# A perceiver layer's attention: TensorE's matmuls split into two streams of 64 rows, and its program written out step by step

## The chip, the core and the metric

One core of a Trainium2 chip runs the whole kernel. The core has five engines that run their own programs and wait for one another through semaphores: TensorE (PE; its weight loads are shown apart, as PEld), VectorE (DVE), ScalarE (ACT), GpSimd (POOL) and SyncE (SP), which here issues all DMAs. The metric is the device time of one execution in microseconds (us); lower is better.

## The reference, cut to what matters

The layer is cross attention, then a recurrent token mixing, then a feed-forward block, each added to the residual. The change touches the attention alone: 32 batches, 64 queries and 1601 context rows of 192 channels each, 16 heads of 64.

```python
q = query @ w_q                      # 32 x 64 x 1024
k, v = split(context @ w_kv)         # 32 x 1601 x 1024 each
scores = einsum('bhqd,bhkd->bhqk', q, k) * 64 ** -0.5
attn = softmax(scores, axis=-1)
out = einsum('bhqk,bhkd->bhqd', attn, v) @ w_out + b_out
x = x + out
```

The kernel never forms k and v. It multiplies the queries by the key weights first (192 channels for each of 16 x 64 head-and-query rows), so the scores are a product of these rows with the raw context, and the attention's output is the probabilities times the raw context, 192 wide, with the value weights applied later. Every operand is held as a high and a low part, and a product is a sum of terms of high and low parts.

## The kernel before, in words

Four stages follow one another: `write_queries` (queries times key weights, to a DRAM scratch), `attend_batches` (the attention), `attention_output` and `mix_and_feed`. The change is in `attend_batches`, which is named p2 in the source.

`attend_batches` takes 256 steps, 8 for each batch; a step handles 128 of the batch's 1024 head-and-query rows. Every engine runs its own program: a first pass of 16 steps, a loop of 14 passes of 16 steps, and a last pass of 16 (`passes`). The order on each engine is fixed by its program.

- TensorE, step s: `step_scores` (L757 to L776), then `product` for step s-4 (L778 to L793). The scores of a step are 128 x 1602, in four banks of PSUM, held once. They are cut into four chunks of 288, 512, 512 and 290 columns, and each chunk is a sum of five matmuls over 128 rows: query parts high and low with channels 0 to 127 of the context's high part, query high with the context's low part, and query high and low with a tile whose rows 0 to 63 are channels 128 to 191 of the high part and whose rows 64 to 127 are the same channels of the low part (the query tile repeats its 64 channels in both halves). The first chunk waits until ScalarE has read the left half of the last scores (`exp_left`), the third until it has read the rest (`exp_done`). The product is 13 tiles of 128 context rows; for each tile the transposed probabilities' high part meets 384 columns (the context's high and low part side by side) and their low part meets 192. Its sums lie in `acc`, one bank for each of two steps in turn.
- VectorE, step s: the maximum of the left half (L714), of the right half (L716), both combined (L719); then for step s-5 the scaled sum of the two halves of `acc` (L695) and its transposition into `o_t` (L701); then, once ScalarE has written the exponentials, their transposition into `turned` (L725), and the reciprocal of the row sums (L726, L728).
- ScalarE, step s: the high part of the landed probabilities of step s-4 (L614, two calls; waits for the end of the product of step s-5, since `pt_hi` and `pt_lo` exist once); the scaled second half of `acc` of step s-5 into `part` (L605); one piece of preparing the next batch; then the two exponentials of step s (L646).
- GpSimd, step s: the low part of the probabilities of step s-4 (L550, two calls), and one piece of preparing the next batch (L558, L562, L569, L577).
- SyncE: for every two steps 16 DMAs that move `turned` into `landed` (L485, `move`), and each batch's loads and stores between them.

## Time and profile before

| | |
|---|---|
| median of 3 runs | 2573.53 us (2570.07 to 2574.76) |
| the profiled execution's own time | 2574.86 us |
| its span, first to last instruction | 2573.1 us |
| mean granted TensorE clock | 0.958 |
| busy: PE, PEld, DVE, ACT, POOL | 2355.1, 2145.3, 1710.9, 1516.0, 1700.7 us |
| 256 steps of the attention, first to last maximum | 170.7 to 2059.3 us of the span |

The page's section 2 shows 40 slices of the span with the busy share of each engine; from the fifth to the thirty-second slice TensorE's digit is 9 throughout at full granted clock. Matmuls are pipelined, so the durations of single matmuls overlap: their rate is read from start to start. The waits and the idle times name the instruction that ended them. A line such as L773 is a line of the kernel before.

### The profile page before, as it was taken

To read this page: it belongs to the slowest core of one execution; us is meant where nothing else is said; L and a number is where in the kernel's file an instruction comes from. 1 tells how busy PE (TensorE), PEld (TensorE's weight loads), DVE (VectorE), ACT (ScalarE), POOL (GpSimd) and SP (SyncE) were. 2 spreads that over 40 slices of the span, in tenths; PEclk is the share of its full clock that TensorE was granted. 3 is DMA by queue.
4 is the path that set the end of the run, shared out by engine and by line. 5 is a ranking of instruction groups with operands and counts; after the bars stand their busy time and mean duration, and the time that the engine had idled before them with its cause. 6 is when DMAs were issued, how large, how long until landed. Compare 5 with 4: busy or idle time off the path is not lost. (4 is left out here: it accounts for less than half of the span.)

```text
span 2573.1 us, 43052 instructions
## 1 busy us (share of the span) xinstructions
PE 2355.1 (92%) x13872; PEld 2145.3 (83%) x13872; DVE 1710.9 (66%) x2666; ACT 1516.0 (59%) x2459; POOL 1700.7 (66%) x873
## 2 busy tenths in 40 slices
PE   4969999999999999999999999999999947855777
PEld 3649999999999999999999999999999945744666
DVE  7766666666666666666666666666666626768762
ACT  4646666666666666666666666666666525543342
POOL 2007788888888888888888888888888632023452
PEclk9989999999999999999999999999999968986888
DMA  5957878888788888888777788878888549910000
GB/s 158 259 155 190 193 193 198 194 192 193 194 192 195 199 194 195 197 198 197 192 193 195 192 193 200 196 192 199 196 198 195 131 102 219 187 50 0 9 9 17
DMA packets 387378, 434.18 MB, mean 169 GB/s; under 512 B 45652, under 2 KB 362232, under 8 KB 387320
## 3 DMA queue, kind: packets, MB, share of 16 engines
q1 hardware_dynamic: 387320, 433.45, 69.2%
q8 instruction: 32, 0.52, 0.1%
q14 instruction: 26, 0.21, 0.0%
HBM read 162.73 MB, written 52.43 MB: 84 GB/s over the span
## 5 line engine op out<-in xcount | busy, mean ns | idle before, releaser
L550 POOL TENSOR_TENSOR p_pt_lo<-p_landed,p_pt_hi 128x768 fp32r<-128x768 f32 (+1 forms) x512 | 1005.1, 1985 | 359.9 <-ACT p_pt_hi L614 359.9
L789 PE MATMUL p_acc<-p_nat,p_pt_hi 128*128 128x384 f32 x3328 | 978.5, 362 | 14.1 <-POOL p_pt_lo L550 13.8
L791 PE MATMUL p_acc<-p_nat,p_pt_lo 128*128 128x192 f32 x3328 | 845.7, 254 | 0.0
L646 ACT ACTIVATE p_prob<-p_scores,p_negmax 128x800 f32<-128x800 f32 (+1 forms) x512 | 471.2, 926 | 515.7 <-DVE p_negmax L719 515.7
L773 PE MATMUL p_scores<-p_ct_hi,p_q_hi 128*128 128x512 f32 (+2 forms) x2048 | 710.2, 350 | 24.2 <-DVE p_ct_hi L746 13.8
L773 PE MATMUL p_scores<-p_ct_hi,p_q_lo 128*128 128x512 f32 (+2 forms) x2048 | 705.1, 348 | 0.0
L725 DVE STREAM_TRANSPOSE turned<-p_prob 128x1664 f32<-128x1664 f32 x256 | 489.5, 1912 | 317.0 <-ACT p_prob L646 317.0
L789 PEld LDWEIGHTS p_acc<-p_nat,p_pt_hi 128*128 128x128 f32 x3328 | 630.7, 190 | 16.5 <-issue 13.7
L791 PEld LDWEIGHTS p_acc<-p_nat,p_pt_lo 128*128 128x128 f32 x3328 | 640.8, 193 | 0.0
L614 ACT ACTIVATE p_pt_hi<-p_landed 128x768 fp32r<-128x768 f32 (+1 forms) x512 | 432.3, 892 | 159.2 <-PE p_acc L791 152.5
L773 PEld LDWEIGHTS p_scores<-p_ct_hi,p_q_hi 128*128 128x128 f32 x2048 | 388.8, 190 | 71.9 <-issue 14.3
L773 PEld LDWEIGHTS p_scores<-p_ct_hi,p_q_lo 128*128 128x128 f32 x2048 | 390.7, 191 | 44.7
L716 DVE TENSOR_REDUCE p_halfmax<-p_scores 128x1 f32<-128x801 f32 x256 | 254.1, 993 | 212.7 <-PE p_scores L773 212.7
L773 PE MATMUL p_scores<-p_ct_lo,p_q_hi 128*128 128x512 f32 (+2 forms) x1024 | 354.2, 346 | 0.0
L714 DVE TENSOR_REDUCE p_halfmax<-p_scores 128x1 f32<-128x800 f32 x256 | 253.7, 991 | 59.5 <-PE p_scores L773 52.3
L773 PEld LDWEIGHTS p_scores<-p_ct_lo,p_q_hi 128*128 128x128 f32 x1024 | 194.3, 190 | 22.3
L577 POOL TENSOR_TENSOR p_nat<-shared,p_nat 128x1152 fp32r<-128x1152 f32 (+1 forms) x62 | 178.5, 2879 | 0.0
L562 POOL TENSOR_TENSOR p_q_lo<-p_stage,p_q_hi 128x1024 fp32r<-128x1024 f32 x62 | 148.5, 2395 | 15.2 <-ACT p_q_hi L624 15.2
L695 DVE SCALAR_TENSOR_TENSOR p_o_q<-p_acc,p_rinv,p_part 128x192 f32<-128x192 f32 x256 | 107.0, 418 | 35.3 <-ACT p_part L605 34.4
L605 ACT ACTIVATE p_part<-p_acc,p_rinv 128x192 f32<-128x192 f32 x256 | 103.0, 402 | 31.4 <-PE p_acc L791 31.4
L558 POOL TENSOR_TENSOR p_ct_lo<-p_stage,p_ct_hi 128x802 fp32r<-128x802 f32 (+1 forms) x62 | 109.5, 1767 | 14.2 <-ACT p_ct_hi L621 14.2
L569 POOL TENSOR_TENSOR p_ct_hi<-p_stage,p_ct_hi 64x802 fp32r<-64x802 f32 (+1 forms) x62 | 109.0, 1757 | 5.6 <-POOL p_pt_lo L550 0.5
(190 smaller groups left out, 2652.9 us busy)
## 6 DMA issues: line engine op xcount, KB each, us to landing
p_landed<-turned SPq DMA_DIRECT2D x2048, 104.0 KB, 2.2
shared<-in_ctx SPq DMA_DIRECT2D x96, 312.0 KB
o_scratch<-shared SPq DMA_DIRECT2D x256, 96.0 KB, 2.6
qk_scratch<-p_out_a SPq DMA_DIRECT2D x16, 1024.0 KB, 4.6
p_oa<-o_scratch SPq DMA_DIRECT2D x32, 512.0 KB, 6.0
p_stage<-qk_scratch SPq DMA_DIRECT2D x31, 512.0 KB, 3.9
p_stage<-qk_scratch SPq DMA_DIRECT2D x62, 256.0 KB, 4.2
p_stage<-in_ctxT SPq DMA_DIRECT2D x31, 401.0 KB, 3.2
```

What stands on the lines that cost most here:

```text
L550: nc.gpsimd.tensor_tensor(pt_lo[:, t0:t1, :, :], by_tile(slot, t0, t1), bits(pt_hi[:, t0:t1, :, :]), ALU.subtract).then_inc(pt_lo_done, 1)
L558: nc.gpsimd.tensor_tensor(ct_lo[1 - par][:, lo:hi], stage[:, u, 0:hi - lo], bits(ct_hi[1 - par][:, 0, lo:hi]), ALU.subtract).then_inc(ct_a ...
L562: nc.gpsimd.tensor_tensor(stepped(q_lo[1 - par][:, u - 3, :]), by_step(stage[:, u - 3, :]), bits(stepped(q_hi[1 - par][:, u - 3, :])), ALU ...
L577: nc.gpsimd.tensor_tensor(x[:, t0:t1, DC:2 * DC], raw[:, t0:t1, :], bits(x[:, t0:t1, 0:DC]), ALU.subtract).then_inc(nat_done, 1)
L614: nc.scalar.activation(pt_hi[:, t0:t1, :, :], by_tile(slot, t0, t1), ACT.Copy).then_inc(pt_hi_done, 1)
L646: nc.scalar.activation(prob[:, lo:hi], scores[:, S0 + lo:S0 + hi], ACT.Exp, bias=negmax[:, par:par + 1], accum_out=rowsum[:, par, h:h + 1] ...
L714: nc.vector.tensor_reduce(halfmax[:, par, 0:1], scores[:, S0:S0 + MID], AX.X, ALU.max, negate=True).then_inc(halfmax_done, 1)
L716: nc.vector.tensor_reduce(halfmax[:, par, 1:2], scores[:, S0 + MID:S0 + NKV], AX.X, ALU.max, negate=True).then_inc(halfmax_done, 1)
L725: nc.vector.transpose(turned[:, j % 4, :], prob[:, :]).then_inc(turned_done, 1)
L773: last = nc.tensor.matmul(scores[:, S0 + lo:S0 + hi], w, x, start=m == 0, stop=m == len(terms) - 1)
L789: nc.tensor.matmul(acc[k % 2][:, 0:2 * DC], pt_hi[:, t, :, :].rearrange("p i x -> p (i x)"), x[:, t, :], start=t == 0, stop=False, skip_gr ...
L791: last = nc.tensor.matmul(acc[k % 2][:, 0:DC], pt_lo[:, t, :, :].rearrange("p i x -> p (i x)"), x[:, t, 0:DC], start=False, stop=t == KT - ...
```

## The change

It touches TensorE's program in `attend_batches`, and what feeds and drains it.

- Scores: the chunks are now 400, 400, 400 and 402 columns, a bank each, and the halves are 800 and 802 columns. A matmul covers 64 rows only: one on rows 0 to 63 (UPPER) into one chunk, and beside it one on rows 64 to 127 (LOWER) into the other chunk of the pair. `passes_of` writes such pairs out: for each pair of chunks five on "their own" halves, then, after a wait for these (`own_done`), four on the crossed halves. The fifth term of the crossed pass (query low with the context's low part of channels 128 to 191) is left out. The order is: own of the left pair, own of the right pair, crossed left (then `left_ready`), crossed right (then `scores_ready`). That makes 36 matmuls for a step in place of 20.
- For this, the tile of channels 128 to 191 holds high and low parts in rows that alternate from chunk to chunk (`ROWS_B`): GpSimd writes the low part in two pieces of 400 columns for each half, and the counts of `ct_b_done` double.
- Product: each of the 26 matmuls becomes two, on rows 0 to 63 and on rows 64 to 127, into two banks: `acc` is now `[P, 2, 512]`, twice. 52 matmuls for a step in place of 26.
- Draining `acc`: VectorE sums its four parts (2 banks x 2 halves of 192) in one `tensor_reduce` of 768 elements, as the first instruction of its step (`sum_out`); ScalarE scales the sum (`scale_out`, now waiting for VectorE and reading SBUF), and VectorE transposes it where it did before (`turn_out`). The old scaled sum (L695) goes.
- TensorE's program is written out for all 256 steps; the other engines keep their loops.

```diff
-HALVES = [(0, 802), (802, NKV + NKV % 2)]
+HALVES = [(0, 800), (800, NKV + NKV % 2)]
...
+    C = HALVES[1][0] // 2
+    CHUNKS = [(0, C), (C, 2 * C), (2 * C, 3 * C), (3 * C, CW)]
+    CHALF, MID = HALVES, HALVES[1][0]
+    PLACE = [512 - C, 512, 3 * 512 - C, 3 * 512]
+    UPPER, LOWER = slice(0, DCB), slice(DCB, P)
+
+    ROWS_B = [(UPPER, LOWER), (LOWER, UPPER)]
...
-        acc = [pb(f"acc{i}", [P, 512]) for i in range(2)]
+        acc = [pb(f"acc{i}", [P, 2, 512]) for i in range(2)]
...
-                    dst = ct_hi[1 - par][DCB:P, 1, lo:hi]
-                    nc.gpsimd.tensor_tensor(dst, stage[DCB:P, u - 6, 0:hi - lo], bits(dst), ALU.subtract).then_inc(ct_b_done, 1)
-                    pool.wait_ge(ct_b_done, n * 2 + (u - 3))
+                    for c in (2 * (u - 6), 2 * (u - 6) + 1):
+                        (c0, c1), rows = CHUNKS[c], ROWS_B[c % 2][1]
+                        dst = ct_hi[1 - par][rows, 1, c0:c1]
+                        nc.gpsimd.tensor_tensor(dst, stage[rows, u - 6, c0 - lo:c1 - lo], bits(dst), ALU.subtract).then_inc(ct_b_done, 1)
+                    pool.wait_ge(ct_b_done, n * 4 + (2 * u - 6))
...
-            def half_out(p, ring, par, fresh):
-
-                act.wait_ge(acc_ready, p + 1)
+            def scale_out(p, ring, fresh):
+
+                act.wait_ge(acc_read, p + 1)
                 act.wait_ge(rinv_done, p + 1)
                 if not fresh:
 
-                    act.wait_ge(acc_read, p)
-                nc.scalar.activation(part[:, :], acc[par][:, DC:2 * DC], ACT.Copy, scale=rinv[:, ring:ring + 1]).then_inc(part_done, 1)
+                    act.wait_ge(o_done, p)
+                nc.scalar.activation(o_q[:, :], o_sum[:, :], ACT.Copy, scale=rinv[:, ring:ring + 1]).then_inc(o_scaled, 1)
...
+            def sum_out(r, j, first):
...
+                dve.wait_ge(acc_ready, p + 1)
...
+                parts = acc[k % 2][:, :, 0:2 * DC].rearrange("p b (h c) -> p c b h", c=DC)
+                nc.vector.tensor_reduce(o_sum[:, :], parts, AX.XY, ALU.add).then_inc(acc_read, 1)
...
             def step(r, j, first):
                 s, par = r * SPP + j, j % 2
+                sum_out(r, j, first)
                 dve.wait_ge(left_ready, s + 1)
...
-                drain(r, j, first)
+                turn_out(r, j, first)
                 dve.wait_ge(exp_done, s + 1)
...
+                def passes_of(chunk_pair, count, own):
+
+                    for m in range(count):
+                        w, x = terms[m]
+                        for rows, c in zip((UPPER, LOWER), chunk_pair):
+                            lo, hi = CHUNKS[c]
+                            last = nc.tensor.matmul(scores[:, PLACE[c]:PLACE[c] + hi - lo], w[rows], x[rows, lo:hi], start=own and m == 0,
+                                                    stop=not own and m == count - 1, skip_group_check=True)
+                    return last
+
+
+                for h in range(2):
+                    if not (first and j == 0):
+
+                        pe.wait_ge(exp_done if h else exp_left, s)
...
+                    passes_of((2 * h, 2 * h + 1), len(terms), True).then_inc(own_done, 1)
+                for h in range(2):
+                    pe.wait_ge(own_done, s * 2 + (h + 1))
+                    passes_of((2 * h + 1, 2 * h), len(terms) - 1, False).then_inc(scores_ready if h else left_ready, 1)
...
+                        for w, width in ((pt_hi, 2 * DC), (pt_lo, DC)):
+                            for i, rows in enumerate((UPPER, LOWER)):
+                                last = nc.tensor.matmul(acc[k % 2][:, i, 0:width], w[rows, t, :, :].rearrange("p i x -> p (i x)"),
+                                                        x[rows, t, 0:width], start=t == 0 and w is pt_hi, stop=t == KT - 1 and w is pt_lo,
+                                                        skip_group_check=True)
...
-            passes(pe, body)
+            for r in range(NB // SPB):
+                body(r, r == 0, r == NB // SPB - 1)
```

## Rows read from the trace of the kernel before

**Rows 1.** Windows, 705 to 1185 us: us, busy by engine (instructions), clock, DMA

```profile
705.00:1185.00 480.00, 480.00 (x2991) 451.60 (x2991) 324.18 (x521) 313.44 (x521) 395.61 (x195) 1.00 0.80 195
```

**Rows 2.** Waits, 400 to 2100 us: engine, line, releaser, us in total, times, longest

```profile
POOL p_pt_lo L550 <- ACT p_pt_hi L614: 320.4, 229, 6.2
DVE p_halfmax L716 <- PE p_scores L773: 187.2, 225, 0.9
```

**Rows 3.** Timeline of PE around one step: start us, duration, line, operation, tiles

```profile
1000.08 0.40 PE L773 MATMUL p_scores<-p_ct_hi,p_q_lo 128*128 128x512 f32 x1
...
1002.18 0.30 PE L773 MATMUL p_scores<-p_ct_hi,p_q_hi 128*128 128x290 f32 x1
...
1002.86 0.34 PE L789 MATMUL p_acc<-p_nat,p_pt_hi 128*128 128x384 f32 x1
...
1006.57 0.32 PE L773 MATMUL p_scores<-p_ct_hi,p_q_hi 128*128 128x288 f32 x1
...
1007.25 0.39 PE L773 MATMUL p_scores<-p_ct_hi,p_q_hi 128*128 128x512 f32 x1
```

**Rows 4.** Timeline of DVE, one step in the steady stretch

```profile
1003.06 0.99 DVE L716 TENSOR_REDUCE p_halfmax<-p_scores 128x1 f32<-128x801 f32 x1 [0.74 <-PE p_scores L773]
...
1006.33 1.92 DVE L725 STREAM_TRANSPOSE turned<-p_prob 128x1664 f32<-128x1664 f32 x1 [1.23 <-ACT p_prob L646]
...
1008.31 0.16 DVE L728 RECIPROCAL p_rinv<-p_rowtot 128x1 f32<-128x1 f32 x1
...
1010.44 0.99 DVE L716 TENSOR_REDUCE p_halfmax<-p_scores 128x1 f32<-128x801 f32 x1 [0.84 <-PE p_scores L773]
```

**Rows 5.** The maxima of the scores, all steps: duration min/median/max, first and last start

```profile
L716 DVE TENSOR_REDUCE p_halfmax<-p_scores x256: 974/992/995, 171.6 to 2059.3; 128x1 f32<-128x801 f32 x128
```

**Rows 6.** Timeline of PEld (weight loads) in the product of the same step

```profile
1003.04 0.19 PEld L789 LDWEIGHTS p_acc<-p_nat,p_pt_hi 128*128 128x128 f32 x1
1003.15 0.19 PEld L791 LDWEIGHTS p_acc<-p_nat,p_pt_lo 128*128 128x128 f32 x1
```

**Rows 7.** Timeline of PE in the first stage: four short matmuls in a row

```profile
40.69 0.60 PE L300 MATMUL p_tp<-p_ident,shared 128*128 128x128 f32 x4
```

**Rows 8.** DMA queues, the program's own instructions among them, 0 to 400 us

```profile
q8 instruction: 14, 0.23, 0.3%
```

**Rows 9.** Timeline of ACT after that product: start, duration, [idle before]

```profile
1006.77 1.69 ACT L614 ACTIVATE p_pt_hi<-p_landed 128x768 fp32r<-128x768 f32 x2 [0.57 <-PE p_acc L791]
```

**Rows 10.** Timeline of POOL, the same time

```profile
1007.69 3.92 POOL L550 TENSOR_TENSOR p_pt_lo<-p_landed,p_pt_hi 128x768 fp32r<-128x768 f32 x2 [1.62 <-ACT p_pt_hi L614]
1011.57 1.61 POOL L558 TENSOR_TENSOR p_ct_lo<-p_stage,p_ct_hi 128x800 fp32r<-128x800 f32 x1
```

**Rows 11.** Timeline of DVE, first steps, where the scores were already there

```profile
170.70 0.98 DVE L714 TENSOR_REDUCE p_halfmax<-p_scores 128x1 f32<-128x800 f32 x1
171.60 0.97 DVE L716 TENSOR_REDUCE p_halfmax<-p_scores 128x1 f32<-128x801 f32 x1
...
193.36 0.16 DVE L728 RECIPROCAL p_rinv<-p_rowtot 128x1 f32<-128x1 f32 x1
193.44 0.97 DVE L714 TENSOR_REDUCE p_halfmax<-p_scores 128x1 f32<-128x800 f32 x1
```

**Rows 12.** Groups by line, whole span: instructions, busy us, mean ns, idle before

```profile
L695 DVE SCALAR_TENSOR_TENSOR p_o_q<-p_acc,p_rinv,p_part 128x192 f32<-128x192 f32 x256 | 107.0, 418 | 35.3 <-ACT p_part L605 34.4
L605 ACT ACTIVATE p_part<-p_acc,p_rinv 128x192 f32<-128x192 f32 x256 | 103.0, 402 | 31.4 <-PE p_acc L791 31.4
...
L637 ACT ACTIVATE p_nat<-shared 128x1152 fp32r<-128x1152 f32 (+1 forms) x62 | 76.7, 1237 | 0.0
```

**Rows 13.** Timeline of SP (DMA issues), one move of two steps

```profile
1030.40 10.41 SPq L485 DMA_DIRECT2D p_landed<-turned  x16
```

**Rows 14.** Waits of SP's DMA queue, 400 to 2000 us

```profile
SPq L480 <- DVE turned L725: 46.2, 53, 1.2
SPq L458 <- POOL p_ct_hi L569: 39.1, 26, 1.7
```

More of the change, by code:

```diff
@@ L650, in drain @@
                 if not (first and j < LAG + 1):
-                    half_out(r * SPP + (j - LAG - 1), (j - LAG - 1) % SB, (j - LAG - 1) % 2, first and j == LAG + 1)
+                    scale_out(r * SPP + (j - LAG - 1), (j - LAG - 1) % SB, first and j == LAG + 1)
             def raise_high(r, j, first):
@@ L688, in _, with turn_out @@
         def _(dve):
-            def out(p, ring, par, fresh_half, first):
-                dve.wait_ge(part_done, p + 1)
-                if not first:
-                    dve.wait_ge(o_done, p)
-                nc.vector.scalar_tensor_tensor(o_q[:, :], acc[par][:, 0:DC], rinv[:, ring:ring + 1], part[:, :], ALU.mult,
-                                               ALU.add).then_inc(acc_read, 1)
-                dve.wait_ge(acc_read, p + 1)
-                if fresh_half is not None:
-                    dve.wait_ge(stored[ring // (SB // 2)], fresh_half)
-                nc.vector.transpose(o_t[:, :, ring, :], o_q[:, :].rearrange("p (k x) -> p k x", x=R)).then_inc(o_done, 1)
-            def drain(r, j, first):
+            def sum_out(r, j, first):
+                if first and j < LAG + 1:
+                    return
+                k = j - LAG - 1
+                p = r * SPP + k
+                dve.wait_ge(acc_ready, p + 1)
+                if not (first and k == 0):
+                    dve.wait_ge(o_scaled, p)
+                parts = acc[k % 2][:, :, 0:2 * DC].rearrange("p b (h c) -> p c b h", c=DC)
+                nc.vector.tensor_reduce(o_sum[:, :], parts, AX.XY, ALU.add).then_inc(acc_read, 1)
+            def turn_out(r, j, first):
                 if first and j < LAG + 1:
@@ L707, in drain @@
                 ring, batch = k % SB, k // SB
-                fresh = ring % (SB // 2) != 0 or (first and batch == 0)
-                out(r * SPP + k, ring, k % 2, None if fresh else (r * SPB + batch) * (16 * G), first and k == 0)
+                dve.wait_ge(o_scaled, r * SPP + (k + 1))
+                if ring % (SB // 2) == 0 and not (first and batch == 0):
+                    dve.wait_ge(stored[ring // (SB // 2)], (r * SPB + batch) * (16 * G))
+                nc.vector.transpose(o_t[:, :, ring, :], o_q[:, :].rearrange("p (k x) -> p k x", x=R)).then_inc(o_done, 1)
             def step(r, j, first):
                 s, par = r * SPP + j, j % 2
+                sum_out(r, j, first)
                 dve.wait_ge(left_ready, s + 1)
-                nc.vector.tensor_reduce(halfmax[:, par, 0:1], scores[:, S0:S0 + MID], AX.X, ALU.max, negate=True).then_inc(halfmax_done, 1)
+                nc.vector.tensor_reduce(halfmax[:, par, 0:1], scores[:, PLACE[0]:PLACE[0] + MID], AX.X, ALU.max, negate=True).then_inc(halfmax_done, 1)
                 dve.wait_ge(scores_ready, s + 1)
-                nc.vector.tensor_reduce(halfmax[:, par, 1:2], scores[:, S0 + MID:S0 + NKV], AX.X, ALU.max,
+                nc.vector.tensor_reduce(halfmax[:, par, 1:2], scores[:, PLACE[2]:PLACE[2] + NKV - MID], AX.X, ALU.max,
                                         negate=True).then_inc(halfmax_done, 1)
@@ L752, in _ @@
             for j in range(LAG + 1):
-                drain(NB // SPB, j, False)
+                sum_out(NB // SPB, j, False)
+                turn_out(NB // SPB, j, False)
         @block.tensor
@@ L760, in step_scores @@
                     pe.wait_ge(q_done, b * 2 + 2)
-                q = lambda t, k: t[par][:, k, (j % SB) * P:(j % SB + 1) * P]
-                for c, (lo, hi) in enumerate(CHUNKS):
-                    if c % 2 == 0 and j % SB == 0:
-                        pe.wait_ge(ct_a_done, b * 2 + (c // 2 + 1))
-                        pe.wait_ge(ct_b_done, b * 2 + (c // 2 + 1))
-                    if c % 2 == 0 and not (first and j == 0):
-                        pe.wait_ge(exp_left if c == 0 else exp_done, s)
-                    ct_a, ct_b, ct_al = (t[:, lo:hi] for t in (ct_hi[par][:, 0, :], ct_hi[par][:, 1, :], ct_lo[par]))
-                    terms = ((q(q_hi, 0), ct_a), (q(q_lo, 0), ct_a), (q(q_hi, 0), ct_al), (q(q_hi, 1), ct_b), (q(q_lo, 1), ct_b))
-                    for m, (w, x) in enumerate(terms):
-                        last = nc.tensor.matmul(scores[:, S0 + lo:S0 + hi], w, x, start=m == 0, stop=m == len(terms) - 1)
-                    if c == 1:
-                        last.then_inc(left_ready, 1)
@@ L788, in product @@
                     for t in range(t0, t1):
-                        nc.tensor.matmul(acc[k % 2][:, 0:2 * DC], pt_hi[:, t, :, :].rearrange("p i x -> p (i x)"), x[:, t, :], start=t == 0, stop=False,
-                                         skip_group_check=True)
-                        last = nc.tensor.matmul(acc[k % 2][:, 0:DC], pt_lo[:, t, :, :].rearrange("p i x -> p (i x)"), x[:, t, 0:DC], start=False,
-                                                stop=t == KT - 1, skip_group_check=True)
+                        for w, width in ((pt_hi, 2 * DC), (pt_lo, DC)):
[3 more added lines that the diff above has]
+                                                        skip_group_check=True)
                 last.then_inc(acc_ready, 1)
```

34 lines of the change are left out of this document (18 added, 16 removed).

## The prediction

> **What bounds the kernel now.** I read the windows first. From 705 to 1185 us TensorE is busy for all 480 us at full granted clock, while VectorE has 324 us, ScalarE 313 us and GpSimd 396 us of work [rows 1]. The waits agree: GpSimd waits for ScalarE's high part and VectorE for the scores, while TensorE has no wait of weight in that stretch [rows 2]. So TensorE's pace is the pace of a step. The timeline shows what it is made of. From start to start, five matmuls of 288 columns take 1007.25 - 1006.57 = 0.68 us, that is 0.136 us each; nine of 512 take 1002.18 - 1000.08 = 2.10, that is 0.2333 each; the five of 290 take 0.68; the product's 13 tiles take 1006.57 - 1002.86 = 3.71, that is 0.2854 for a pair of 384 and 192 columns [rows 3]. The sum is 0.68 + 2.33 + 0.68 + 3.71 = 7.40 us; from one right-half maximum to the next it is 1010.44 - 1003.06 = 7.38 [rows 4]. All 256 steps run from 171.6 to 2059.3 us, 7.40 for one on average [rows 5], so this stage is 1888 us of the 2573.1.
>
> Two things in these rows matter for a cut into halves. A weight load costs 0.107 to 0.11 us from start to start (1003.04 to 1003.15) [rows 6], and four loads with matmuls of 128 columns come at the same pace: (0.60 - 0.27) / 3 = 0.11, taking 0.27 for the last one's own length [rows 7]. Under a matmul of 290 columns or more it hides; under one of 192 it does not quite. The excess over pure streaming is small everywhere.
>
> **TensorE after the change.** Scores: 18 pairs of 64-row matmuls of 400 columns. Between 0.136 at 288 and 0.2333 at 512 the slope is 0.000434 us for a column, so a full-height matmul of 400 columns would take 0.185 [rows 3]. If the two of a pair run side by side, a step's scores cost 18 x 0.185 = 3.33 us against 3.69 now: one tenth of the columns goes with the term that is left out, and two starts in twenty. The product keeps its columns: 26 pairs in place of 26 matmuls, 3.71 us. Sum 7.04. If the two run one after the other, it is twice that, 14.1. No row of before shows a matmul on half the rows, so these are the bounds. I take 7.04: the two use different rows of the array, different partitions of the operands and different banks, and no row shows something that they share except the order of issue and the port for weights.
>
> That port is the doubtful place. There are 88 loads in a step where there were 46. If the loads of both halves stand in one line at 0.107, a pair of the scores takes 0.214 (over 0.185) and a tile of the product 4 x 0.107 = 0.428 (over 0.285): 18 x 0.214 + 13 x 0.428 = 9.42 us. The same price comes out if the queue can't issue a load and a matmul faster than the 0.11 us of [rows 7]; that row can't say whether it shows a limit of the load or of the issue.
>
> The Trainium skill, TensorEngine Tiling (Array Packing), Key Properties, says that different tiles "can execute LdWeights and Matmul in parallel"; no run here shows it yet. By that rule the loads of the halves don't line up, and 7.04 stands. The skill's page TensorE: Matmul & The Clock Gate (Part 3, The mechanism) says that a load overlaps matmuls in flight only where the row groups differ. By that rule a full-height load could not hide now, and the split would gain all of it; the rows disagree, since loads of all 128 rows start 0.11 us apart under running matmuls [rows 6], so nothing is to be gained there.
>
> **TensorE's program, written out.** The loop's back edge costs nothing visible now, since TensorE is busy throughout [rows 1]. Written out, the program has to be fetched while it runs: in the first 400 us, 14 blocks of 16 KB came in [rows 8] for the written-out parts, and the mean step shows no room for a stall with each. A step has 88 matmuls and 88 loads in place of 46 and 46, so a block (256 instructions of 64 bytes) would last some 10 us in place of 20. I cost it at nothing, and at up to 1 us for a block (every 1.4 steps) if each one stalls: 0.7 us a step.
>
> **Who is next at 7.04.** Four loops of dependences close once in a step.
>
> GpSimd and ScalarE around the product. `pt_hi` and `pt_lo` exist once. The product ends at 1006.57, ScalarE starts at 1006.77 [rows 9], GpSimd at 1007.69, and the second low half is ready at 1011.61 [rows 10]: 5.04 us after the product's end. Then 7 of 13 tiles are left, 7 x 0.2854 = 2.00. The loop needs 7.04, and up to 0.1 more for the wake-ups.
>
> VectorE. Its chain goes from the right-half maximum over the maximum of both, ScalarE's exponentials and the transposition to the reciprocal: 1008.31 - 1003.06 = 5.25 us [rows 4]. The reciprocal to the next instruction, unwaited, is 0.08, and left-half to right-half maximum is 0.90 when the scores are there [rows 11]. Without any wait for TensorE that is 6.23, and this is why VectorE could wait 0.83 us in each step [rows 2, 4]. The change adds `sum_out` to that chain, in front. The scaled sum (0.42 us [rows 12]) that it replaces ran while VectorE waited 1.23 us for the exponentials anyway [rows 4], so its going gives nothing back. `sum_out` reads 768 elements of PSUM in one reduction; the nearest row is a reduction of 800, which occupies 0.90, so 0.87. Bounds: 0.42 below (no cheaper than the sum it replaces) and 4 x 0.42 = 1.67 above (each of four parts at the old price). The chain needs 6.23 + 0.87 = 7.10, with bounds 6.65 and 7.90. The skill's tiling page (PSUM Bottleneck) warns that a faster TensorE moves the limit to the draining of PSUM; that agrees with this sum, which alone gives the number.
>
> SyncE. A move of two steps takes 10.4 us of issue [rows 13] of 14.8. Over 1600 us its queue waited 46.2 + 39.1 us [rows 14], that is 0.39 for each of 217 steps: it can't go below 7.38 - 0.39 = 6.99.
>
> ScalarE has one new wait, `scale_out` on `sum_out`; queued behind it are a piece of preparation (up to 1.24 us [rows 12]) and the exponentials. `sum_out` ends 5.25 + 0.08 + 0.87 = 6.20 us after a right-half maximum, the scaling (0.40 [rows 12]) and the preparation end by 7.84, and the next exponentials are due at 7.10 + 1.2 = 8.3 (1.2 is 1006.33 - 1003.06 less the wait of 1.23 and twice 0.42 for L695 and the transposition behind it [rows 4, 12]). It has cover of about 0.4 us; if that were gone, the excess would go on VectorE's chain one for one. The split of GpSimd's low part for channels 128 to 191 adds two starts in a batch, hidden beside its idle time [rows 2].
>
> **The sum.** The loops need 7.04, 7.04 to 7.14, 7.10 and 6.99 us. The largest likely one is 7.10 to 7.14, and loops this close will jostle: I take 7.15. Against 7.38 that is 0.23 us for each of 255 steps, 59 us. The last step's drain gets 0.5 longer. Span 2573.1 - 58 = 2515; its own time lies 1.8 above the span, and the median of the runs 1.3 below that: 2515 for the median.
>
> **Rivals.**
> 1. *The other loops take the gain.* If the wake-ups, the fetches or a late DMA cost 0.1 to 0.25 us more, a step takes 7.25 to 7.4: 2545 to 2578 us. For it: four loops within 0.15 us. Against it: the mean of all steps now lies only 0.02 above a steady one [rows 4, 5], so stalls are rare.
> 2. *VectorE's new reduction is slow (the other side).* Place: `sum_out`, at the head of VectorE's step. It decides from 7.38 - 6.23 = 1.15 us upward. At its upper bound, 1.67, a step takes 7.90: 2573.5 + 255 x 0.52 = 2706 us. A partial overlap of the halves would look alike in time and reach 2700 to 2750.
> 3. *Loads or issue in one line (slower).* 9.42 us: 2573.5 + 255 x 2.04 = 3094 us.
> 4. *The change doesn't do what it says:* the halves exclude each other, 14.1 us, 2573.5 + 255 x 6.7 = 4280 us.
>
> **How the numbers follow.** My forecast (7.05 to 7.25 us a step, 2490 to 2545) has 0.67; rival 1 has 0.10, of which 0.03 lies within 0.2% of before; rival 2 with partial overlap 0.07, with 0.01 of it within 0.2%; rival 3 has 0.12 and rival 4 0.04. Bound 0.2% is about what a measurement of this kernel can tell from no change. Faster 0.67 + 0.07 = 0.74, same 0.04, slower 0.22. The range runs from 2480 (7.02 a step, TensorE alone) to 2690, past rival 1 and through most of rival 2: it leaves out rivals 3 and 4 and a rest, just under 2 in 10. Its own range is 2490 to 2545.
>
> **What would show it.** Right: the two matmuls of a pair start within a few hundredths of a us and pairs of 400 columns come every 0.18 to 0.19 us, tiles every 0.285; `sum_out` near 0.96 us by its row; VectorE's wait in front of L716's successor shrinks from 0.83 to under 0.1, and TensorE for the first time waits in each step, for GpSimd's low part or the exponentials, by about 0.1 us. Rival 1 shows as larger waits of TensorE, or gaps that the profile puts down to issue at even distances of one block. Rival 2 shows as a row of `sum_out` over 1.2 us with VectorE never waiting. Rival 3 shows as loads 0.107 apart without a gap, whichever half they are for, and pairs at 0.21; rival 4 as the second of each pair starting when the first is through. The prediction is wrong at its root if pairs don't overlap, and wrong in size if the loops' slack, which I read from single steps, isn't there.

## The result and the profile after

| | before | after |
|---|---|---|
| median of the runs | 2573.5 us | 2641.3 us (2639.0 to 2646.0, 4 runs) |
| profiled execution: time, span | 2574.9, 2573.1 us | 2639.0, 2637.2 us |
| ratio after : before | | 1.027, interval 1.0255 to 1.0285 |
| mean step, first to last right-half maximum | 7.40 us | (2116.5 - 170.4) / 255 = 7.63 us |
| TensorE busy, 705 to 1185 us | 480.0 us | 464.4 us |

The change is 68 us slower, where 58 us less was forecast. Of the 64 us by which the span grew, 58 lie between the first and the last of the 256 maxima.

TensorE does what was hoped. The timeline of TensorE in the scores of a step (start, duration, "x2" is one pair) shows the halves side by side:

```profile
1004.62 0.37 PE L782 MATMUL p_scores<-p_ct_hi,p_q_hi 64*128 64x400 f32 x2
1004.82 0.34 PE L782 MATMUL p_scores<-p_ct_hi,p_q_lo 64*128 64x400 f32 x2
1005.01 0.34 PE L782 MATMUL p_scores<-p_ct_lo,p_q_hi 64*128 64x400 f32 x2
...
1007.75 0.35 PE L782 MATMUL p_scores<-p_ct_hi,p_q_hi 64*128 64x400 f32 x2
```

From the start of the first pair to that of the last are 17 pairs in 3.13 us: 0.184 us for a pair (0.185 was taken from [rows 3]). But the engine is no longer busy throughout. The windows view of 705 to 1185 us (columns as in [rows 1]) has 15.6 us without a matmul, and GpSimd and ScalarE do less work in the same time, so fewer steps:

```profile
705.00:1185.00 480.00, 464.38 (x5562) 443.68 (x5564) 337.35 (x505) 311.08 (x505) 387.71 (x207) 1.00 0.78 191
```

The waits of 400 to 2100 us (as [rows 2]: us in total, times, longest) have one kind that was next to nothing before, ScalarE's high part waiting for the landing of a move; TensorE's new waits come behind it. Before, then after:

```profile
ACT p_pt_hi L614 <- DMA p_landed<-turned: 1.7, 2, 1.0
```

```profile
ACT p_pt_hi L619 <- PE p_acc L813: 173.6, 144, 3.9
ACT p_pt_hi L619 <- DMA p_landed<-turned: 130.7, 79, 3.3
DVE p_halfmax L722 <- PE p_scores L782: 89.6, 163, 1.6
...
PEld p_acc L813 <- issue: 78.7, 88, 2.6
PE p_acc L813 <- POOL p_pt_lo L553: 54.0, 60, 2.3
```

SyncE's own queue, 400 to 2000 us, had 46.2 and 39.1 us of waiting before [rows 14] and has half of that now, although it has no issue more to make:

```profile
SPq L483 <- DVE turned L733: 20.0, 24, 1.1
SPq L488 <- POOL p_pt_lo L553: 16.7, 36, 0.7
SPq L461 <- POOL p_ct_hi L574: 4.3, 7, 2.8
```

One stall in full, around 410 us, on SyncE, ScalarE, GpSimd and TensorE ([idle before <- what ended it]):

```profile
395.55 1.98 SPq L497 DMA_DIRECT2D o_scratch<-shared  x4
397.76 11.53 SPq L488 DMA_DIRECT2D p_landed<-turned  x16
...
412.20 1.69 ACT L619 ACTIVATE p_pt_hi<-p_landed 128x768 fp32r<-128x768 f32 x2 [2.46 <-DMA p_landed<-turned]
413.12 3.89 POOL L553 TENSOR_TENSOR p_pt_lo<-p_landed,p_pt_hi 128x768 fp32r<-128x768 f32 x2 [3.15 <-ACT p_pt_hi L619]
415.06 0.21 PEld L813 LDWEIGHTS p_acc<-p_nat,p_pt_hi 64*128 64x128 f32 x2 [1.74 <-issue]
415.09 0.44 PE L813 MATMUL p_acc<-p_nat,p_pt_hi 64*128 64x384 f32 x2 [1.44 <-POOL p_pt_lo L553]
```

The move's sixteen issues take 11.53 us where one took 10.41 before [rows 13]. It lands late, ScalarE has idled 2.46 us, GpSimd 3.15, and TensorE stands for 1.44 us. What the profile puts down to "issue" for TensorE is mostly this: the weight load beside that matmul has the same gap under that name, and of the 76 us that such loads waited from 400 to 2000 us, 66 stand beside a matmul's wait for GpSimd's low part.

A long stand has a second price. Five times between 400 and 2000 us the granted clock falls to half (1.2 in place of 2.4 GHz) for 3.4 us, each time within 1.5 us behind a stand of TensorE of 1.7 to 2.3 us (four other stands of 1.8 to 2.1 us brought none). That is 17 us at half clock, where the kernel before has none in this stretch, and so at most some 9 us of the loss.

What lengthens the issues is in the page's third section, the queue by which the program's own instructions come in blocks of 16 KB. Before, then after:

```profile
q8 instruction: 32, 0.52, 0.1%
```

```profile
q8 instruction: 192, 3.15, 0.6%
```

Between 400 and 2000 us it is 3 blocks before (all behind 1950 us, near the last pass) and 145 after, one in 11 us. In the same stretch 143 of SyncE's DMA issues took over 0.7 us (4 before), in total 110 us over the usual 0.602 (2 before), and they begin 0.16 us (median) behind the start of a block: nearly every block lengthens one issue, by 0.8 us on average. The distribution of the move's issues (ns, minimum/median/maximum) shows it as a maximum only, since nine of ten are untouched:

```profile
L488 SPq DMA_DIRECT2D p_landed<-turned x1677: 585/602/1903, 399.8 to 1999.3; - x187
```

### The profile page after: what moved, and what is told of

It reads as the page before. It is cut to its first block and busy times, and to the rows that moved or that the text cites. A ratio compares the mean times of both kernels' runs of the same rounds, so it can differ in the third digit from the quotient of the medians.

```text
span 2637.2 us, 64213 instructions
## 1 busy us (share of the span) xinstructions
PE 2345.9 (89%) x24624; PEld 2169.6 (82%) x24624; DVE 1800.6 (68%) x2668; ACT 1542.9 (59%) x2459; POOL 1712.8 (65%) x935
## 3 DMA queue, kind: packets, MB, share of 16 engines
q8 instruction: 192, 3.15, 0.6%
## 5 line engine op out<-in xcount | busy, mean ns | idle before, releaser
L813 PE MATMUL p_acc<-p_nat,p_pt_hi 64*128 64x384 f32 x6656 | 1038.6, 370 | 84.7 <-POOL p_pt_lo L553 80.3
L813 PE MATMUL p_acc<-p_nat,p_pt_lo 64*128 64x192 f32 x6656 | 883.7, 252 | 0.0
L813 PEld LDWEIGHTS p_acc<-p_nat,p_pt_hi 64*128 64x128 f32 x6656 | 671.7, 188 | 165.4 <-issue 108.6
L782 PE MATMUL p_scores<-p_ct_hi,p_q_hi 64*128 64x400 f32 (+1 forms) x4096 | 689.5, 346 | 24.3 <-DVE p_ct_hi L755 14.1
L813 PEld LDWEIGHTS p_acc<-p_nat,p_pt_lo 64*128 64x128 f32 x6656 | 680.8, 191 | 0.0
L782 PE MATMUL p_scores<-p_ct_hi,p_q_lo 64*128 64x400 f32 (+1 forms) x3072 | 547.2, 343 | 0.0
L782 PEld LDWEIGHTS p_scores<-p_ct_hi,p_q_hi 64*128 64x128 f32 x4096 | 402.0, 185 | 26.7 <-issue 15.1
L782 PE MATMUL p_scores<-p_ct_lo,p_q_hi 64*128 64x400 f32 (+1 forms) x2048 | 363.6, 342 | 0.0
L782 PEld LDWEIGHTS p_scores<-p_ct_hi,p_q_lo 64*128 64x128 f32 x3072 | 307.4, 187 | 0.0
L705 DVE TENSOR_REDUCE p_o_sum<-p_acc 128x192 f32<-128x768 f32 x256 | 244.8, 956 | 52.8 <-PE p_acc L813 46.3
```

Source lines behind the costliest of these rows:

```text
L705: nc.vector.tensor_reduce(o_sum[:, :], parts, AX.XY, ALU.add).then_inc(acc_read, 1)
L782: last = nc.tensor.matmul(scores[:, PLACE[c]:PLACE[c] + hi - lo], w[rows], x[rows, lo:hi], start=own and m == 0, stop=not own and m == cou ...
L813: last = nc.tensor.matmul(acc[k % 2][:, i, 0:width], w[rows, t, :, :].rearrange("p i x -> p (i x)"), x[rows, t, 0:width], start=t == 0 and ...
```

## The experiments

Theory A: the blocks by which the written-out program is fetched lengthen SyncE's DMA issues, and through late landings the steps. Its rivals, by the letters that the expectations use: B (each block stalls TensorE itself; from e6 on the same is called D, which also takes in any other harm of a block), and C (the halves or the new draining are at fault, for instance because closely matched loops jostle, and writing out costs nothing). Ratios are to the kernel before on the same chip.

### Writing out, alone and taken back

e1: the changed kernel, TensorE in a loop of 16 steps again.

```diff
-            for r in range(NB // SPB):
-                body(r, r == 0, r == NB // SPB - 1)
+            passes(pe, body)
```

> The changed kernel with TensorE's loop put back (14 passes of 16 steps), all else kept. Theory A: the blocks of TensorE's written-out program that are fetched while it runs hold up SyncE's DMA issue (146 blocks between 400 and 2000 us, 143 issues of over 0.7 us there, 118 us more than 0.602 us each), and SyncE's line of issues is what a step waits for. If the loop's body of some 2900 instructions stays in place, the blocks and the long issues go, a step takes the 7.2 to 7.3 us of the undisturbed steps, and the kernel 2530 to 2550 us. If the body is fetched anew in each pass, the blocks stay at 0.69 a step and the time at 2640, which says nothing against A. Theory B, that each block stalls TensorE itself and SyncE's delay only follows from the longer step: the same time as A, but with the long issues still there. Theory C, the halves or the new reduction cost the time, not the fetches: 2640 with the blocks gone.

Measured: 2711.7 us, 1.055 (1.053 to 1.057), slower still. The loop doesn't take the blocks away: there are 230. Its body of 16 steps has 16 x 176 = 2816 matmuls and loads where that of before has 16 x 92 = 1472, and the 176 blocks that come between 400 and 2000 us say that it is fetched anew in each pass. New is a wait of TensorE at the back edge, about twice in a pass (waits, 400 to 2100 us):

```profile
PEld p_scores L782 <- issue: 79.6, 26, 4.2
PE p_scores L782 <- issue: 71.0, 26, 3.8
```

The stands at the back edge also bring stretches at half the granted clock, 99 us in the 1600 from 400 to 2000 us. So writing out was better than the loop for this body, by 70 us, and the experiment says nothing against A.

e2: the kernel before with TensorE's program written out, and nothing else (the same edit the other way round).

> The kernel before, with TensorE's program written out for all steps and nothing else changed. 93 instructions a step make 0.36 blocks a step. Theory A: each block makes one DMA issue some 0.8 us longer, 0.29 us a step, which fits into the 0.39 us a step that SyncE's queue waited before: the step stays at 7.38 to 7.42 us, the kernel at 2573 to 2590 us, and SyncE's waits shrink to about 0.1 us a step. Theory B, a block stalls TensorE by 0.5 to 1 us: TensorE is the bound here, so 93 blocks cost 45 to 90 us, 2620 to 2665 us. Theory C: no change, 2573.

Measured: 2591.1 us, 1.0069 (1.0052 to 1.0086): 18 us for the writing out alone. 108 blocks in all, 77 of them between 400 and 2000 us, 72 issues of SyncE over 0.7 us, and ScalarE waits for landings (waits, 400 to 2100 us):

```profile
ACT p_pt_hi L614 <- DMA p_landed<-turned: 46.9, 37, 3.0
```

C, by which writing out is free (2573), and B (2620 to 2665) are both out. A's size fits, 1 us above its range.

### The stores off SyncE's queue

e3 (changed kernel), e6 (e2), e7 (before) and e8 (e5, below): the eight stores of a batch are issued by ScalarE, one behind the exponentials of each step.

```diff
-                    if not begins:
-                        store(n - 1, 0)
...
                     step(r, j, first)
+                    store_after(n, u, begins, first and j == SB)
```

> The changed kernel, written out as it is, but the 8 stores of each batch to the scratch are issued by ScalarE, one behind the exponentials of each step, in place of SyncE. Theory A: SyncE's line gets 8 issues of 0.48 us shorter for a batch, 0.49 us a step, so it needs 7.46 - 0.49 = 6.97 to 7.1 and the other loops decide: 7.25 to 7.35 us a step, 2540 to 2570 us, although as many blocks are fetched as before. Theory B: 2640, since TensorE's own stalls stay. Theory C: 2640.

> The kernel before (full-height matmuls), TensorE's program written out as in e2_before_written_out, and the eight stores of each batch issued by ScalarE in place of SyncE. Theory A: the blocks come as in e2, but SyncE's queue has lost 8 issues of some 0.6 us in a batch of 59 us, so its spare grows from 61 to some 180 us in 1600 and the stalls shrink: 2573 to 2583 us, against 2591 with the stores on SyncE. Theory D (a block holds TensorE itself, whatever SyncE does): as e2, 2588 to 2594 us.

> Control: the kernel before with its loop and with the eight stores of each batch issued by ScalarE. SyncE had spare and TensorE was busy throughout in the kernel before, so theories A and D both expect no change: 2570 to 2577 us. Were it faster by more than 5 us, the stores on SyncE would cost something of their own, and e3 and e6 would not speak on the fetches alone.

Measured: e3 2595.7 us, 1.0083 (1.0063 to 1.0102), 46 us less than the changed kernel with the same 192 blocks, where B and C expected no gain; e6 2583.9 us, 1.0036 (1.0023 to 1.0049), 7 us less than e2; e7 2570.0 us, 0.9987 (0.9977 to 0.9998), so the place of the stores as such is worth 3 us at most. SyncE now waits 135 us of 1600 in e3, thus has spare, and landings are still late (78.5 us). e6 came 1 us above A's range and e3 26 above it: spare in the queue isn't enough. That led to the slack of the single move, below.

### The scores alone in halves

e4: the product with 128 rows and the old draining; scores in halves; written out.

```diff
-                        for w, width in ((pt_hi, 2 * DC), (pt_lo, DC)):
-                            for i, rows in enumerate((UPPER, LOWER)):
...
...
+                        nc.tensor.matmul(acc[k % 2][:, 0:2 * DC], pt_hi[:, t, :, :].rearrange("p i x -> p (i x)"), x[:, t, :], start=t == 0, stop=False,
```

> The changed kernel with the scores in halves, but the product with matmuls over all 128 rows into one bank, and its two halves scaled and added by ScalarE and VectorE as before the change (no reduction of 768). Written out. 62 matmuls a step, 0.49 blocks. Theory A: SyncE needs 6.99 + 0.49 x 0.83 = 7.40 us a step, so 2575 to 2590 us. Theory B (TensorE 7.04 plus 0.49 blocks at 0.5 to 1 us): 7.3 to 7.5, 2550 to 2605, with the waits on TensorE's side. Theory C, the reduction on VectorE is what costs: VectorE's chain is back at 6.23, TensorE at 7.04 to 7.1, 2500 us. If going from 64-row to 128-row matmuls and back twice a step costs TensorE anything, its gaps show at the two borders of a product.

Measured: 2601.4 us, 1.0107 (1.009 to 1.0124). That is 11 us above A's range, and far above the 2500 that stood for a reduction at fault. With 140 blocks it lies between e2 and the changed kernel, but its undisturbed step is 7.39 us, not the 7.04 that the streams add up to. The weight loads show where it goes, at the first load of each kind:

```profile
1001.65 0.19 PEld L778 LDWEIGHTS p_scores<-p_ct_hi,p_q_hi 64*128 64x128 f32 x2 [0.16 <-issue]
1005.13 0.19 PEld L807 LDWEIGHTS p_acc<-p_nat,p_pt_hi 128*128 128x128 f32 x1 [0.27 <-issue]
```

Those two gaps a step are not in the changed kernel, where everything has 64 rows. From start to start each of the two borders costs the matmuls about 0.18 us, together the 0.35 us that were missing. The Trainium skill, TensorEngine Tiling (Array Packing), Key Properties, says "Mode switching requires drain"; the trace agrees, at about 0.16 and 0.27 us.

### The same work without the blocks

e5: the changed kernel with TensorE in a loop of 8 steps (1408 matmuls and loads), which needs fixed buffers. It leaves out the turning of the buffers: TensorE computes every batch from the first batch's context and queries, so its output is not the layer's. Number and shape of instructions, waits and transfers are kept. The same holds for its descendants e8, e12, e14 and e18.

```diff
...
-                          (q_hi[par][:, 0, at], ct_lo[par]), (q_hi[par][:, 1, at], ct_hi[par][:, 1, :]),
...
+                          (q_hi[0][:, 0, at], ct_lo[0]), (q_hi[0][:, 1, at], ct_hi[0][:, 1, :]),
...
-            for r in range(NB // SPB):
-                body(r, r == 0, r == NB // SPB - 1)
+            batch(0)
+            with pe.Fori(1, NB) as b:
+                batch(b)
```

> The changed kernel with its halves, but TensorE's program is a loop over batches again, with a body of one batch (8 steps, some 1500 instructions, as long as the body that stayed resident in the kernel before). To make this possible TensorE reads the context and the queries always from the first of their two buffers while all writers write the second, so every batch is computed from the first batch's context and queries; the number and shape of all instructions, waits and transfers is that of the changed kernel. Theory A (the 16 KB blocks by which TensorE's written-out program is fetched lengthen SyncE's DMA issues, and SyncE's queue is then too slow for the moves): no blocks between 400 and 2000 us, no DMA issue over 0.7 us, moves of 10.3 us, steps of 7.1 to 7.3 us with few stalls, 2525 to 2555 us. Theory C (the stalls belong to the halves: closely matched loops jostle once a step takes 7.1 us, whatever is fetched): blocks gone, stalls as in the changed kernel, 2620 to 2650 us.

> e5_short_loop with the eight stores of each batch issued by ScalarE (again every batch uses the first batch's context and queries). Theory A in its plain form: without fetches SyncE needs 7.0 us a step and VectorE 7.1 to 7.2, so the relief moves little: within 15 us of e5, at 2520 to 2550 us. If SyncE were the bound at 7.1 us even without fetches (theory A2), it would be faster than e5 by over 15 us.

Measured: e5 2547.1 us, 0.9903 (0.9886 to 0.9919); e8 2549.6 us. Same halves, same draining, same transfers, 94 us less than the changed kernel and 26 less than before. From 400 to 2000 us there is no block of TensorE's queue, no stretch at half clock, no issue of a move over 0.672 us, and in the waits of 400 to 2000 us those for landings are gone:

```profile
ACT p_pt_hi L619 <- DMA p_landed<-turned: 2.4, 3, 0.9
```

This settles C against A: all 94 us hang on how TensorE's program is fetched. It also gives the price of a step without it, 7.27 us on the mean of 255, and e8 shows that SyncE's load isn't what sets these 7.27 (A2 is out).

How little a block must cost to matter is read from SyncE's and ScalarE's timelines of e5:

```profile
1186.95 0.54 SPq L468 DMA_DIRECT2D p_stage<-in_ctxT  x1
1187.72 10.35 SPq L488 DMA_DIRECT2D p_landed<-turned  x16
...
1200.45 1.69 ACT L619 ACTIVATE p_pt_hi<-p_landed 128x768 fp32r<-128x768 f32 x2 [0.68 <-PE p_acc L813]
```

The last of the sixteen is issued from 1197.46 to 1198.07. The trace has its landing at 1200.1, and ScalarE starts at 1200.45, so this move behind loads has 0.3 us of slack, and a block in it adds 0.8. Over all moves from 400 to 2000 us the time from the last landing to ScalarE's start is 0.9 us at the median in e5, and under 0.35 in one of ten; in the kernel before it is 1.3 and 0.9. That goes with what a block costs in the two: 18 us for e2's 108 blocks, 0.17 each, and 94 for the changed kernel's 192, 0.49 each.

### A shorter move, all blocks kept

e9, e11 and e12: the changed kernel, the kernel before and e5, with 4 of a move's 16 DMAs issued by ScalarE behind the exponentials of the next step (e10: and the stores too).

```diff
-                for i in range(G):
+                for i in range(G if whole else G - 1):
...
                     step(r, j, first)
+                    move_rest(r, j, first)
```

> The changed kernel (halves, TensorE's program written out, its 192 blocks as before), with 4 of the 16 DMAs of every move issued by ScalarE behind the exponentials of the step that follows, and 12 by SyncE. Theory A, made more precise: a block costs time only because it lengthens a DMA issue of a move, and the move of two steps (11 to 11.7 us of issue and 2.5 us to land, of 14.5 us) then lands after ScalarE wants it; TensorE itself is never short of instructions. Then a move that is issued in some 8 to 9 us absorbs its blocks: ScalarE's wait for the landing falls from 131 us to under 25 in 1600, the steps are 7.1 to 7.3 us, and the time is 2545 to 2560 us, all blocks still there. Theory D (a block also starves TensorE or slows something else): 2590 to 2620 us, with TensorE's waits put down to issue as large as in the changed kernel (74 us).

> Control: the kernel before (loop, full-height matmuls) with 4 of the 16 DMAs of every move issued by ScalarE. TensorE is busy throughout there, so both theories expect no change: 2569 to 2577 us.

> e5_short_loop (halves, TensorE's loop of 8 steps, so no blocks; every batch computed from the first batch's context and queries) with 4 of the 16 DMAs of every move issued by ScalarE. If GpSimd's and ScalarE's loop around the product is what sets 7.26 us without fetches, and not the moves: within 5 us of e5, 2542 to 2552 us. If the moves' latency set it, 2515 to 2535 us.

> As e9_move_quarter_on_act, and the eight stores of each batch on ScalarE's queue as well. Theory A: SyncE's queue has then 62 issues in a batch where it had 86, nothing is late, and the time is within 10 us of e9: 2543 to 2556 us. If the order of the stores among the moves still made landings late in e9, this one is faster than e9 by over 10 us. Theory D: 2585 to 2615 us.

Measured: e9 2603.3 us (1.0118), e11 2598.8 (1.0109), e12 2577.1 (1.0013); e10 2728.2 (1.062). In e9 the waits for landings are gone from the list, but the controls e11 and e12, which were expected to stay as they were, are 27 and 30 us slower than without the edit. ScalarE's queue and its work in e12:

```profile
1209.63 1.26 ACTq L646 DMA_DIRECT2D p_landed<-turned  x2
...
1211.57 0.63 ACTq L646 DMA_DIRECT2D p_landed<-turned  x1
1212.31 1.69 ACT L619 ACTIVATE p_pt_hi<-p_landed 128x768 fp32r<-128x768 f32 x2 [0.93 <-PE p_acc L827]
```

The issues run beside the exponentials, but the next instruction of ScalarE starts only behind the fourth, 0.10 us behind its end in each of the 108 moves from 400 to 2000 us, and four reach just past the point at which the high part is due: it starts 0.57 us behind the product's last matmul, 0.35 in e5. A block now lengthens these, and holds ScalarE (e9, waits of 400 to 2000 us, a kind that e12 does not have):

```profile
ACT p_pt_hi L619 <- issue: 28.7, 14, 2.5
```

So the comparison of e9 with e12 (26 us) could not tell A from D. e10 was expected within 10 us of e9 and came 125 above: with a store behind the four, ScalarE waited 190 us of 1600 for its own issues.

e13 to e15 had the same four as two in each of two steps:

> The changed kernel, written out, with 4 of the 16 DMAs of a move issued by ScalarE, but now two behind the exponentials of each of the two steps that follow, in place of four behind those of the first. In e12 the four took 2.5 us from the first exponential's start, 0.1 to 0.2 us past the point at which ScalarE wants to begin the next high part; two take 1.25 us (some 2.1 with a block), which the exponentials (1.95 us) and the wait behind them cover. Theory A (late landings are the only link between the blocks and the time): no landing is late, ScalarE is not held, 2547 to 2565 us with all 192 blocks, thus faster than the kernel before. Theory D (the blocks also hold TensorE, or another engine): 2585 to 2610 us.

> Control without blocks: e5_short_loop (TensorE's loop of 8 steps; every batch computed from the first batch's context and queries) with the same placement as e13. Covered as worked out there: 2543 to 2553 us, like e5 (2547). Were it like e12 (2577), ScalarE's issues cost time by their number, wherever they stand.

> Control: the kernel before with the same placement. If it is covered, 2570 to 2578 us; if ScalarE's issues cost time by their number, 2590 to 2600 us, as with four behind one step (2599).

Measured: e13 2784.9 us (1.083), e14 (as e5) 2714.4 (1.055), e15 (as before) 2732.5 (1.062). My placement was wrong: the second pair is issued a step later and lands late even without blocks (182 us of waits for landings in e14). They tell nothing on A and D, but show what late landings cost: e14 lies 167 us above e5, with 53 of 1600 us at half the granted clock.

e16: only 2 of the 16 on ScalarE, both in the first step. e17 and e18 (as e5) have the stores on ScalarE as well, two in each odd step.

```diff
-                    for g in range(G):
+                    for g in range(G if whole or i < G - 1 else 2):
...
+                for g in range(2, G):
...
+                    act.dma_start(dst, turned[i * R:(i + 1) * R, slots, g * GK:(g + 1) * GK]).then_inc(moved[par], 16)
```

> The changed kernel, written out, with 2 of the 16 DMAs of a move issued by ScalarE behind the exponentials of the first step that follows, 14 by SyncE. Without blocks (e5) a move that stands behind loads ends its issue at 1198.07 us, lands some 2.3 us later, and ScalarE's high part starts at 1200.45: a slack of about 0.1 us, and a block (+0.8 us) is late in full. With 14 issues the move ends 1.3 us earlier, and a block fits into the slack. ScalarE's two take 1.25 us (2.1 with a block) from the first exponential, 2.6 us ahead of the next high part. SyncE's queue: 78 issues of 0.65 and 5.5 blocks of 0.8 us are 55 of 58 us. Theory A: 2555 to 2580 us. Theory D (the blocks cost time in another way too): 2600 to 2625 us.

> As e16_move_eighth_on_act, and the eight stores of a batch too are issued by ScalarE, two in each odd step, so that ScalarE has two issues in every step and SyncE 70 in a batch, 46 us and 4.4 us of blocks of 58. Theory A: 2548 to 2565 us with all 192 blocks, faster than the kernel before (2573). Theory D: 2590 to 2620 us.

> Control of e17 without blocks: TensorE's loop of 8 steps (every batch computed from the first batch's context and queries), with e17's placement of the issues. ScalarE's two issues are covered in each step: 2542 to 2552 us, like e5 (2547). If it is above 2560, the placement has a price of its own, which is to be taken off e17.

Measured: e16 2553.8 us, 0.993 (0.9908 to 0.9951): 88 us less than the changed kernel, 21 less than before, and 7 above e5. It has all the blocks (first line, page), and the same lengthening of issues: from 400 to 2000 us 121 of SyncE's took over 1.0 us, 127 in the changed kernel. But SyncE is through with a move 1.3 us sooner, and hardly a landing is late (waits, 400 to 2000 us):

```profile
q8 instruction: 192, 3.15, 0.6%
```

```profile
1189.62 9.07 SPq L488 DMA_DIRECT2D p_landed<-turned  x14
```

```profile
ACT p_pt_hi L619 <- PE p_acc L827: 142.4, 204, 2.0
...
ACT p_pt_hi L619 <- DMA p_landed<-turned: 19.6, 15, 2.0
PEld p_acc L827 <- issue: 17.1, 41, 1.3
```

That decides A against D: 192 blocks cost 94 us where a move behind loads has 0.3 us of slack and 7 us where it has 1.3 more, and TensorE's "issue" waits and the stretches at half clock go with them. One control is missing: no run has e16's placement without the blocks. The placement could hide a larger cost of the blocks only by a gain of its own, and in e5 there are but 2.4 us of waits for landings to be gained.

e17 and e18 were expected at 2548 to 2565 and 2542 to 2552 and came to 2634.2 and 2630.1 us (1.0237 and 1.0219): they differ by 4 us, and both lose some 80 us to something of the placement. It is a stall of ScalarE once in each pass of 16 steps, in e18 for example

```profile
1262.35 1.68 ACT L615 ACTIVATE p_pt_hi<-p_landed 128x768 fp32r<-128x768 f32 x2 [4.68 <-issue]
```

behind the last exponentials of a pass. The stalls are 13 in 1600 us, 63.5 us in all, and with each the granted clock goes to half for 3.4 or 6.8 us, 82 us in all. The pages have a row that goes with them, the instruction blocks of 8 KB on another queue than TensorE's, in e5 and then in e18:

```profile
q14 instruction: 27, 0.21, 0.0%
```

```profile
q14 instruction: 91, 0.75, 0.1%
```

In e18 they come five in a pass, at the same places in each; three of them in the example start at 1258.0, 1260.8 and 1262.9 us, two of these within the stall. So here it looks as if ScalarE's own loop, lengthened by the issues, no longer stays in place and is fetched anew, as TensorE's was in e1. No run tested it, and e10, with more issues on ScalarE, has 27 of these blocks.

## Why the prediction was wrong, step by step

**The halves.** Right. Pairs run side by side, 0.184 us for 400 columns; tiles take 0.286 to 0.289 (0.2854 taken); loads of both halves don't line up. The shortest steady steps of e5 are 7.03 to 7.09 us where 7.04 was worked out. Rivals 3 and 4 fall.

**VectorE.** Right. `sum_out` occupies 0.956 us by its row, 0.96 was expected, and the first step of rival 2 (1.15 us) is far. Over e5's 1600 us VectorE still waits 25 us for the scores.

**The loop of `pt_hi` and `pt_lo`.** Right as the loop that binds without blocks, too short by 0.2 us: 7.27 in place of 7.04 to 7.14. In e5 the product's last tile gives way to the next pair at 1185.58, ScalarE starts at 1185.85 and the second low half is ready at 1186.77 + 3.93 = 1190.70, that is 5.12 us where 5.04 was taken. TensorE, which has stood, starts the tile 0.15 us later, needs 0.33 for it and 1.72 for the other six, which makes 7.32 in this step. The gap was seen as a risk ("up to 0.1 for the wake-ups") and belongs to a loop that never had to wait before, so no row of before had it. It is 0.12 us over the 7.15 that I chose, 31 us of time: e5 is at 2547 where 2515 was forecast. This is rival 1 in kind and size, though in e5 alone.

**The program written out.** This is the step that failed. I costed the fetches at nothing, with a bound of 1 us a block for a stall of *TensorE*, and left out whom else a block can touch. In the changed kernel TensorE is not short of instructions (its waits are for GpSimd); SyncE, whose DMA issues share the time with the blocks, loses 0.8 us for each. And the upper bound of 0.7 us a step stood beside the sum but had no chance of its own among the rivals (rival 1 has the fetches at 0.25 at most), though it would have given 7.85 us a step. The mean came to 7.63 - 7.27 = 0.36 us a step from this alone, 92 us, which is the difference between the changed kernel and e5 (94).

**SyncE.** I took its loop from the queue's waits, 7.38 - 0.39 = 6.99 us, as a floor that doesn't move [rows 14]. Two things were missing. 5.5 blocks in a batch take 0.8 each, 0.55 us a step, which lifts the floor to 7.54, above the 7.15 that I chose. And a queue's spare isn't the slack of one transfer: a move behind loads needs 10.4 us of issue [rows 13] and 1.6 to 2.1 more until the last has landed (e5), out of the two steps that it has, and this sum was not made. e3 showed the first (46 us back), e16 the second (88 us back).

**The side.** The likeliest case had the right engine at the right pace; of its gain of 59 us, 31 went with the loop of `pt_hi` and `pt_lo`, and a term that stood at zero took the rest and 68 more. That 2641 us still lies between 2480 and 2690 is luck: that width was kept for a slow `sum_out` or halves that overlap in part, and neither came.

## What to carry to other kernels

Before writing a loop out or lengthening its body, count its instructions against a body that is known to run without blocks, and if it will be fetched, ask which DMA issues have no slack, on every engine's queue and not on the one whose program grows. For a chain of transfers work out the slack of the single one (ready, issue, landing, wanted), not the share of time that the queue is busy. Where a transfer is cut into many issues on one queue, one or two of them on a second engine can buy the slack, as long as they end before that engine's next urgent instruction; check it against a control that has the edit and not the cause.

## What the runs showed of the hardware

- A block of 16 KB of one engine's program lengthens a DMA issue on another engine's queue by about 0.8 us (0.602 to 1.4 us; up to 1.9 to 2.2 for a move's). It does so on SyncE's queue (143 of 2248 issues in the changed kernel) and on ScalarE's: in e9 24 of its 424 issues took over 1.0 us, each during a block, in e12, without blocks, none of 432 over 0.9. By which path it does that no run shows.
- With a quarter of each move on ScalarE, 76 of SyncE's issues took over 0.7 us, up to 1.0 (e12); none did in e5 and in e8, all three without blocks of TensorE's queue. That it comes from two engines issuing moves at once is not shown.
- A body of 1408 to 1472 matmuls and loads ran without blocks (e5, before), one of 2816 was fetched in every pass and cost up to 4.2 us at the back edge (e1). The Trainium skill, Advanced Engine Details and Errata, section ISA Cache, gives 128 KB on TensorE and 16 KB for 256 instructions (an estimate from that: 2048 instructions); these runs agree on both sides of it.
- The Trainium skill, DMA: Bandwidth & Descriptors, section Issuing engines are not separate DMA queues, says that a second issuing engine only saves the time to initiate, "usually small relative to the DMA itself". Here sixteen issues in a row are the larger part (10.4 us, where one DMA lands 2.2 us after its issue began, at the median), and moving two of them to ScalarE was worth 88 us.
- ScalarE issues DMAs beside its own running instruction (0.62 us each), but doesn't begin the next one until they are handed over (e12: 0.10 us behind the fourth issue).
- Behind stands of TensorE of 1.7 to 2.3 us the granted clock fell to half (1.2 GHz) for 3.4 us, five times in 1600 us of the changed kernel, and four like stands passed without. With the stands of 3.3 to 4.1 us in e18 it fell each time, for 3.4 to 6.8 us, and for up to 10.2 us in e1.
